# A one-core graph-attention layer: a fourth group of 512 columns turned by DMA, GpSimd's subtraction in quarters, 1 MB loads and another order of exp

## What is computed

```python
q = x @ Wq.T + bq
k = x @ Wk.T + bk
v = x @ Wv.T + bv
scores = q @ k.T / sqrt(128)
scores = where(adj > 0, scores, -9e15)
att = softmax(scores, axis=-1) @ v
att = elu(att)
out = layernorm(x + att, axis=-1, eps=1e-5)
```

## Time and profile before

| | us |
|---|---|
| median of 3 runs | 457.14 |
| the profiled execution | 456.9 |
| span of its trace | 455.1 |
| mean granted TensorE clock | 0.998 |

### The profile page before, as it was taken

The page is one execution under the profiler, slowest core; times in us unless marked ns, Lnnn a source line. Parts: engine busy times, 40 slices in busy tenths (PEclk is TensorE's granted clock), DMA queues, the critical chain, the costliest instruction groups (busy, mean ns, idle before and its releaser), DMA issues.

```text
span 455.1 us, 11786 instructions
## 1 busy us (share of the span) xinstructions
PE 441.7 (97%) x3596; PEld 326.7 (72%) x3596; DVE 376.7 (83%) x665; ACT 354.9 (78%) x643; POOL 273.9 (60%) x426
## 2 busy tenths in 40 slices
PE   7998999999999999999999999999999999999984
PEld 5574677777777777777777777777777777777763
DVE  0678889888898889889898889989898888988633
ACT  3767677778788777778878787778878787777892
POOL 0055336776666666776666666676666666677563
PEclk9999999999999999999999999999999999999999
DMA  8934999899999999999989999999999999995341
GB/s 223 353 94 131 194 238 268 197 257 215 248 234 234 239 213 216 239 241 212 258 229 233 239 225 235 203 252 222 245 225 237 232 227 232 211 254 120 71 78 40
DMA packets 128444, 96.90 MB, mean 213 GB/s; under 512 B 103344, under 2 KB 112048, under 8 KB 128432
## 3 DMA queue, kind: packets, MB, share of 16 engines
q1 hardware_dynamic: 128000, 96.55, 88.4%
q10 hardware_dynamic: 432, 0.20, 0.2%
HBM read 69.47 MB, written 2.10 MB: 157 GB/s over the span
## 4 chain that ended last, share of the span: by engine, by line
PE 90%; ACT 3%; DMA 3%; POOL 2%; issue 1%; SPq 0%; POOLq 0%; DVE 0%; ACTq 0%
PE ps_out L702 23%; PE ps_t L679 14%; PE ps_out L704 12%; PE ps_scores L665 12%; PE ps_scores L664 12%; PE ps_scores L663 12%; PE ps_t L607 2%; DMA p_turned<-p_rows 2%; PE ps_out L618 2%; PE ps_out L607 1%; DMA x_rows<-in_x_dram 1%; ACT scores L399 1%; PE ps_scores L629 1%; ACT p_rows L416 1%; POOL p_rows L289 1%
## 5 line engine op out<-in xcount | busy, mean ns | idle before, releaser
L512 DVE CUSTOM_DVE_ANT_0 scores<-ps_scores,adj 128x1024 f32<-128x1024 f32 x128 | 155.8, 1217 | 1.8 <-issue 0.5
L527 DVE TENSOR_TENSOR p_lo<-ps_t,p_hi 128x512 f16<-128x512 f32 x160 | 108.6, 688 | 49.6 <-ACT p_hi L408 44.5
L408 ACT ACTIVATE p_hi<-ps_t 128x512 f16<-128x512 f32 x160 | 94.8, 593 | 68.6 <-PE ps_t L679 66.5
L399 ACT ACTIVATE scores<-scores,neg_max 128x1024 f32<-128x1024 f32 x128 | 145.8, 1139 | 0.1
L702 PE MATMUL ps_out<-v_parts,p_hi 128*128 128x257 f16 x640 | 124.8, 274 | 0.9 <-DVE p_lo L527 0.8
L704 PE MATMUL ps_out<-v_parts,p_lo 128*128 128x129 f16 x640 | 116.1, 218 | 0.0
L289 POOL TENSOR_TENSOR p_rows<-scores,p_rows 128x1024 f16<-128x1024 f32 x64 | 106.2, 1659 | 11.3 <-ACT p_rows L416 11.3
L498 DVE TENSOR_SCALAR adj<-adj 128x1024 f32<-128x1024 int32 x128 | 108.5, 848 | 0.0
L679 PEld LDWEIGHTS ps_t<-ident,scores 128*128 128x128 f32 x640 | 79.1, 141 | 34.4 <-ACT scores L399 5.4
L679 PE MATMUL ps_t<-ident,scores 128*128 128x128 f32 x640 | 96.4, 273 | 3.3 <-ACT scores L399 3.2
L663 PE MATMUL ps_scores<-k_hi,q_hi 128*128 128x512 f16 x256 | 96.7, 378 | 0.5 <-DVE max_parts L512 0.5
(11 more groups left out here) (70 smaller groups left out, 407.6 us busy)
## 6 DMA issues: line engine op xcount, KB each, us to landing
adj<-in_adj_dram SPq DMA_DIRECT2D x128, 512.0 KB, 4.9
out_dram<-y_out SPq DMA_DIRECT2D x32, 64.0 KB, 4.5
x_rows<-in_x_dram SPq DMA_DIRECT2D x3, 512.0 KB, 6.5
p_turned<-p_rows SPq DMA_TRANSPOSE x64, 5.3
x_rows<-in_x_dram SPq DMA_DIRECT2D x2, 256.0 KB, 3.9
w_rows<-in_L_gnn_Wk_dram ACTq DMA_DIRECT2D x1, 64.0 KB, 2.8
w_rows<-in_L_gnn_Wq_dram ACTq DMA_DIRECT2D x1, 64.0 KB, 3.4
w_rows<-in_L_gnn_Wv_dram ACTq DMA_DIRECT2D x1, 64.0 KB, 3.9
```

The costliest lines, as they stand in the source:

```text
L399: nc.scalar.activation(s_sb[s][:, cols], s_sb[s][:, cols], ACT.Exp, bias=neg_max[:, s:s + 1]).then_inc(exp_done, 1)
L408: nc.scalar.activation(p_hi[:, k, :], ps_t[bank_of(s, g)][:, :], ACT.Copy).then_inc(phi_ready, 1)
L512: nc.vector.tensor_tensor_reduce(out=s_sb[s][:, cols], in0=ps_scores[c % 2][:, :], in1=mask_sb[s][:, cols], scale=SCALE, scalar=-3.0e38, o ...
L527: nc.vector.tensor_tensor(p_lo[:, k, :], ps_t[bank_of(s, g)][:, :], p_hi[:, k, :], ALU.subtract).then_inc(plo_ready, 1)
```

## The change

- `DMA_COLS` becomes 1024 and 1024, so group 3 goes the DMA's way and TensorE turns groups 4 to 7. `T_AT`, `PV_ORDER` and `EXP_ORDER` are set anew: exp runs over pieces 2, 0, 1, 3, and `values` takes groups 4 to 7 first.
- `low_rows` makes each subtraction in four instructions of 256 columns.
- `adj` is loaded in halves of 2048 columns (1 MB); the second half of tile p+1 and the first of tile p+2 are asked for in period p, each behind a DMA transpose.
- `turn` of `c = 1` is issued one period later in SP's order, at the head of a period.
- ACT's `high_rows` move to j = 4 and 6, its end-of-tile steps to j = 1, 3, 5, 7.
- POOL's order is `finish_att`, `low_rows` 0, `finish_y`, `finish_mean`, `low_rows` 1, `finish_norm`.
- DVE finds the row maximum before the mask piece that follows; one mask piece moves to the next period.
- At the start: 12 warm-up transposes for 9, and `x` in six chunks for five.

```diff
-DMA_COLS = (PIECE, BANK,)
+DMA_COLS = (PIECE, PIECE)
-T_AT = {3: 4, 4: 6, 5: 7, 6: 8, 7: 10}
-PV_ORDER = (3, 4, 5, 6, 0, 7, 1, 2)
+T_AT = {4: 3, 5: 5, 6: 8, 7: 9}
+PV_ORDER = (4, 5, 6, 7, 0, 1, 2, 3)
+EXP_ORDER = (2, 0, 1, 3)
+LOW_PARTS = 4
-WARM_UP = 9
-X_CHUNKS = ((0, 1), (1, 2), (2, 4), (4, 6), (6, 8))
+WARM_UP = 12
+X_CHUNKS = ((0, 1), (1, 2), (2, 3), (3, 4), (4, 6), (6, 8))
...
+            def load_half(i, slot, h, first):
                 if not first:
-                    sp.wait_ge(masked_ready, PIECES * (i - 2) + c + 1)
+                    sp.wait_ge(masked_ready, PIECES * (i - 2) + 2 * h + 2)
+                cols = slice(2 * h * PIECE, 2 * (h + 1) * PIECE)
+                sp.dma_start(adj_sb[slot][:, cols], adj_tiled[i, :, cols]).then_inc(adj_in[slot][h], 16)
...
# SP, period(p, n)
-                load_piece(p + 1, 1 - n, 3), store(p - 4, n), load_piece(p + 2, n, 0), load_piece(p + 2, n, 1)
-                turn(p - 1, 1 - n, 0), load_piece(p + 2, n, 2), turn(p - 1, 1 - n, 1)
+                turn(p - 2, n, 1), load_half(p + 1, 1 - n, 1), store(p - 4, n)
+                turn(p - 1, 1 - n, 0), load_half(p + 2, n, 0)
...
# POOL
-                nc.gpsimd.tensor_tensor(p_rows[c][:, w:], s_sb[s][:, c * PIECE:c * PIECE + w], p_rows[c][:, 0:w],
-                                        ALU.subtract).then_inc(rows_lo, 1)
+                for b in range(LOW_PARTS):
+                    cols = slice(b * w // LOW_PARTS, (b + 1) * w // LOW_PARTS)
+                    last = nc.gpsimd.tensor_tensor(p_rows[c][:, w:][:, cols], s_sb[s][:, c * PIECE:c * PIECE + w][:, cols],
+                                                   p_rows[c][:, 0:w][:, cols], ALU.subtract)
+                last.then_inc(rows_lo, 1)
...
# POOL, period(p, n)
-                    finish_y(p - 3, 1 - n, first)
+                    finish_att(p - 3, 1 - n)
                     low_rows(p - 1, 1 - n, 0)
-                    finish_norm(p - 3, 1 - n)
+                    finish_y(p - 3, 1 - n)
+                    finish_mean(p - 3, 1 - n)
                     low_rows(p - 1, 1 - n, 1)
+                    finish_norm(p - 3, 1 - n, first)
...
# ACT, period(p, n)
-                    if j == 0 and has_3:
-                        attention(p - 3, 1 - n)
-                    if j == 2 and has_1:
+                    if j == 4 and has_1:
                         high_rows(p - 1, 1 - n, 0, not warm and p == 1)
-                    if j == 4 and has_1:
+                    if j == 6 and has_1:
                         high_rows(p - 1, 1 - n, 1, not warm and p == 1)
                     if j % 2 == 1 and has_1:
-                        exp_piece(p - 1, 1 - n, j // 2)
-                    if j == 2 and has_3:
+                        exp_piece(p - 1, 1 - n, EXP_ORDER[j // 2])
+                    if j == 1 and has_3:
+                        attention(p - 3, 1 - n)
+                    if j == 3 and has_3:
                         elu_exp(p - 3, 1 - n)
-                    if j == 4 and has_3:
+                    if j == 5 and has_3:
                         row_sum(p - 3, 1 - n)
-                    if j == 6 and has_3:
+                    if j == 7 and has_3:
                         square_sum(p - 3, 1 - n)
...
# DVE, period(p, n)
+                    if j == 7 and has_scores:
+                        row_max(p, n)
-                        if makes_mask:
-                            mask_piece(p + 1, 1 - n, j // 2)
+                    if j == 1 and has_scores:
+                        mask_piece(p, n, 3)
+                    if j in (3, 5, 7) and has_scores and makes_mask:
+                        mask_piece(p + 1, 1 - n, j // 2 - 1)
...
# PE, period(p, n)
-                    if j < 7 and has_2:
-                        values(p - 2, n, PV_ORDER[j + 1], False)
-                    if j == 7 and has_1:
-                        values(p - 1, 1 - n, PV_ORDER[0], not warm)
+                    if has_2:
+                        values(p - 2, n, PV_ORDER[j], first)
```

More of the change, by code:

```diff
@@ L121, in attention_kernel @@
         v_lo = sem("v_lo")
-        adj_in = [[sem(f"adj_in{n}_{c}") for c in range(PIECES)] for n in range(2)]
+        adj_in = [[sem(f"adj_in{n}_{h}") for h in range(2)] for n in range(2)]
         mask_ready = sem("mask_ready")
@@ L191, in exp_count @@
         def exp_count(i, c):
-            return PIECES * i + c + 1
+            return PIECES * i + EXP_ORDER.index(c) + 1
         def bank_of(s, g):
@@ L209, in _ @@
             sp.dma_start(bv_rows[:, :], bv.rearrange("(a d) -> a d", a=1).to_broadcast([P, D])).then_inc(bv_in, 16)
[L211 removed]
+            def load_half(i, slot, h, first):
                 if not first:
[L214 to L216 removed]
+                    sp.wait_ge(masked_ready, PIECES * (i - 2) + 2 * h + 2)
+                cols = slice(2 * h * PIECE, 2 * (h + 1) * PIECE)
+                sp.dma_start(adj_sb[slot][:, cols], adj_tiled[i, :, cols]).then_inc(adj_in[slot][h], 16)
             def load(i, slot):
[L219 to L220 removed]
+                for h in range(2):
+                    load_half(i, slot, h, True)
             def store(i, slot):
@@ L230, in turn, with period @@
                 sp.dma_start_transpose(p_turned[c][s][:, :, :], p_rows[c][:, :]).then_inc(turned[c], 16)
-            def period(p, n, head=True, turns=True, stores=True, loads=True):
+            def period(p, n, head=True, turns_0=True, turns_1=True, stores=True, loads=True):
+                if turns_1:
+                    turn(p - 2, n, 1)
                 if head:
-                    load_piece(p + 1, 1 - n, 3, False)
+                    load_half(p + 1, 1 - n, 1, False)
                 if stores:
                     store(p - 4, n)
[L238 to L242, removed]
+                if turns_0:
                     turn(p - 1, 1 - n, 0)
                 if loads:
-                    load_piece(p + 2, n, 2, False)
-                if turns:
-                    turn(p - 1, 1 - n, 1)
+                    load_half(p + 2, n, 0, False)
             load(0, 0)
             load(1, 1)
-            period(0, 0, head=False, turns=False, stores=False)
-            period(1, 1, stores=False)
+            period(0, 0, head=False, turns_0=False, turns_1=False, stores=False)
+            period(1, 1, turns_1=False, stores=False)
             period(2, 0, stores=False)
@@ L260, in _ @@
             period(TILES, 0, head=False, loads=False)
-            period(TILES + 1, 1, head=False, turns=False, loads=False)
+            period(TILES + 1, 1, head=False, turns_0=False, loads=False)
             store(TILES - 2, 0)
@@ L317, in finish_norm @@
                                         ALU.add).then_inc(pool_done, 1)
+            def finish_norm(i, s, first):
+                one = slice(s, s + 1)
+                base = POOL_OPS * i
                 pool.wait_ge(sqsum_ready, i + 1)
@@ L324, in finish_norm @@
                 pool.wait_ge(pool_done, base + 10)
+                if not first:
+                    pool.wait_ge(stored[s], 8 * (i - s))
                 nc.gpsimd.tensor_tensor(y_out[:, s, :], centred[:, s, :], rstd[:, one].to_broadcast([P, D]),
@@ L575, in period @@
                             low_part(p - 1, 1 - n, g)
+                    if j % 2 == 1 and has_scores:
+                        masked_piece(p, n, j // 2, not warm and p < 2)
+                    if j == 7 and has_scores:
+                        row_max(p, n)
                     if j == 7 and has_2 and not last:
                         reciprocal(p - 2, n)
-                    if j % 2 == 1 and has_scores:
-                        masked_piece(p, n, j // 2, not warm and p < 2)
-                        if makes_mask:
-                            mask_piece(p + 1, 1 - n, j // 2)
-                    if j == 7 and has_scores:
-                        row_max(p, n)
+                    if j == 1 and has_scores:
+                        mask_piece(p, n, 3)
+                    if j in (3, 5, 7) and has_scores and makes_mask:
+                        mask_piece(p + 1, 1 - n, j // 2 - 1)
             for n in range(AHEAD):
                 low_of_projection(n)
-                if n >= AHEAD - PIECES:
-                    mask_piece(0, 0, n - AHEAD + PIECES)
+                if n > AHEAD - PIECES:
+                    mask_piece(0, 0, n - AHEAD + PIECES - 1)
             period(0, 0, has_1=False, has_2=False, warm=False)
@@ L706, in values, with period @@
                 last.then_inc(pv_done, 1)
-            def period(p, n, has_scores=True, has_1=True, has_2=True, warm=True):
+            def period(p, n, has_scores=True, has_1=True, has_2=True, warm=True, first=False):
                 for j in range(STEPS):
@@ L732, in _ @@
             pe.wait_ge(v_lo, STEPS)
-            period(2, 0)
+            period(2, 0, first=True)
             period(3, 1)
```

18 lines of the change are left out of this document (9 added, 9 removed).

## The result

The changed kernel takes 535.77 us (median of 4 runs, 535.07 to 536.91) where the kernel before takes 457.10. The ratio is 1.173, 95% interval 1.170 to 1.175: 79 us slower. The prediction was 519.3 us, with a range of 488 to 544. The trace shows the loop that it forecast. A fall of TensorE's clock, which it didn't name, adds 22 us, and smaller errors the other way take 5 us off; so the sum is 18 us short.

The account below looks back on a forecast made before the run. PE's stream, 12.76 us a period, was taken as the bound. high_rows 0 ending at 68.5, 28 turns of 14.77, one of 14.13, then 15.4 and 5.65 gave a span of 517.3, so 519.3 us; range 488 to 544.

Parts of the forecast that it names:

- The turn: From ACT's high_rows 0 through POOL's quarters, y, row_sum and PE back to high_rows 0: 14.13 us, 14.77 with a meeting.
- the meeting: On POOL, a mask piece waits for the last quarter and holds res back by 0.64 us a turn.
- POOL's other stretch: low_rows 1, the norm, att, then elu_exp: some 0.2 us under the turn, adding nothing.
- the other three mask pieces: On DVE beside POOL: they fall into POOL's gaps or its 0.2 us of slack.
- The last turn: At the end of the loop, where no mask is made: one turn of 14.13 us.
- PE's own period: PE's stream alone would need 12.32 us a period, against 12.76 before.
- The gain of the moved group: One group of transposes per tile leaves PE: 0.44 us, 32 times, 14.1 us if nothing else got late.
- Quarters: POOL's four 256-column instructions per subtraction: 2.58 us, bounds 2.14 and 2.80.
- The start: Smaller x chunk saves 0.8 us of PE's wait; period 3 begins at 60.8 us.
- PE as the bound: Rival: ACT takes the wait in its stride and PE's 12.32 us stays the period; 445.1 us, chance 0.08.
- Late loads: Rival: adj's 1 MB load behind a transpose lands late, costing about 1 us a period; 548 us, chance 0.07.
- the second rival: Mask pieces and quarters on POOL: no meeting, 501.4 us, or two, 537; 0.64 us each a turn; chance 0.27.

Follow-up runs that it names:

- e1: The changed kernel with one move on GpSimd, finish_y ahead of the first low_rows: 442.4 us, ratio 0.971 to the kernel before.
- e3: The changed kernel with 16 dummy transposes of the identity on TensorE before it waits for exp of piece 3: 515.3 us.
- e5: The changed kernel with each low_rows subtraction as one instruction of 1024 columns, no quarters: 496.8 us.
- e2: The changed kernel with ACT's row_sum moved behind the second high_rows at j = 6: 486.7 us.
- e9: e3 with mask piece 1 of every tile cut to 8 of its 1024 columns, so it computes something else: 503.0 us.
- e7: e1 with 9 warm-up transposes for 12, x still in six chunks: 443.6 us.

## Why the prediction was right, and where its size was off

**The turn: right in its order, and partly lucky in its length.** The deciding step, that the subtraction ahead of `y` closes a turn through ACT and POOL that is longer than PE's own stream, is shown by e1: moving that one call opens it. TensorE's way around was 14.77 in the sum; the trace gives 14.53, of which 0.44 is the meeting, so 14.09 for 14.13 without it. But the fast turns are 14.68 to 14.74, because POOL's other stretch closes them. The prediction had that stretch 0.2 us under TensorE's and counted the other three mask pieces into gaps and slack. Two of them lengthen it by 0.48 and 0.44, and it ends 0.15 us later instead. That the whole turn is within 0.1 of 14.77 is two errors that cancel: a meeting put 0.2 too high, and 0.15 of the others left out. The last turn, 13.67 us, is no measure of the 14.13: TensorE makes no scores in it, and part of it is at the low clock (in e3 it is 13.30).

**The range: luck in part.** Its upper end, 544, was made from a second meeting and quarters of 0.70 us. What took the time from 513 or so up to 535.8 was the clock, for which the range had nothing.

**PE's own period: right.** 12.32 counted, 12.31 in e1. The gain of the moved group, 0.45 us a period or some 13 us, exists and is about what e1 is faster than the kernel before (13.6).

**Quarters: right in size, and worse than the sum says in effect.** 2.56 for 2.58 (its own terms add up to 2.57). The cost of the meeting was 0.44 for 0.64. The sum let the mask piece run for its whole 0.69 behind the quarter, and `res` for its whole 0.46 behind the piece; in the trace the quarter ends at 317.51, the piece 0.55 later and `res` 0.31 after that. The rule of the Trainium skill that I weighed ("SBUF — State Buffer", "SBUF: two separate sides": an exclusive lock for the whole instruction) agrees with the second subtraction of e5, which a mask piece waits out to its end. What I drew from it, 0.64 on POOL's path for each piece that quarters let in, does not: the second subtraction loses 0.48 us with quarters, and undivided POOL loses 0.45 in `var` behind it. The quarters cost by their own 0.42 us.

**The clock: missed.** The sum has no term for it, though it says that PE waits 2 to 3 us a period. 15 turns of the 29 are 1.5 us longer by it: 22 us. I had taken that TensorE's clock stays where it was, as in the kernel before, whose page has no slice under 9; but that kernel's PE never stood still in the steady state, so its trace couldn't tell. e3 shows it: with the wait filled, 20.5 us go.

**The start: too careful.** Period 3 began at 58.2 us (59.53 of ACT's first copy in it, less 1.36), not 60.8. Setting the terms side by side: start -2.6, turns at the full clock -2.1, clock +22.4, tail +0.1; 17.8 us together, from a span of 517.3 to 535.1. Without the clock's term, the changed kernel would take some 513 us; e3, where the clock stays up, takes 515.3.

**The rivals.** PE as the bound (445.1 us) did not occur in the changed kernel; its number is nearly that of e1, for which it was in effect worked out. Late loads did not occur: a load of 1 MB lands in 5.7 us (median) instead of the 9.8 I allowed:

```profile
adj<-in_adj_dram SPq DMA_DIRECT2D x64, 1024.0 KB, 5.7
```

A second and a third meeting did occur, on POOL's other stretch: they cost 0.15 us a turn, not the 0.64 of the second rival, because most of their length falls into the slack of that stretch.

**What stays open.** Why the clock falls in every second turn or so and not in all. All 14 waits of 2.09 us and more (up to 2.42) were followed by a slow stretch, but of the 15 waits from 1.96 to 2.04 us only two were: the length of the wait goes with it and doesn't decide it alone. In e2 and e5, with waits of 1.2 to 1.6 us in the steady state, it never fell there. The share of the smaller `x` chunk at the start is open too.

## What to carry to other kernels

When a reordering puts a long operation of engine B ahead of a short one that engine A waits for, look for the loop before looking at busy shares: write down one full turn with start-to-start spacings, and compare it with the period of the bound engine. An engine's idle time is slack only for a chain that doesn't pass through the waits it is made of. Where two ways around are within a few tenths of a microsecond of each other, count the waits on both: small delays on the shorter one can make it the longer. And give TensorE's clock a term of its own as soon as a change lets TensorE stand still for some 2 us in each period; a wait of 2 us then cost 3.5 in this kernel, while waits of 1.2 to 1.6 cost only themselves.

## What the runs showed of the hardware

- The granted clock fell to 0.51 behind idle stretches of 2.0 to 2.4 us in half of the periods; a window of 3.5 us held 19 matmuls there and 32 at the full clock. The 29 turns hold 16 slow stretches, 14 of them behind a wait of 2.09 us or more. With 16 dummy transposes in the gap (0.4 us of idle left) it stayed up.
- Four subtractions of 256 columns on GpSimd take 2.56 us from end to end, one of 1024 takes 2.14.
- A mask piece of VectorE that meets a GpSimd instruction lengthens the next one by 0.44 us, whether that is `res` (the changed kernel; 0.46 without the piece in e9) or `expm1` (e5). Behind an undivided subtraction the piece itself took 1.47 us instead of 0.69.
- The trace's record of the granted clock begins at 13.3 us in the kernel before and at 7.7 in e7, where TensorE's pace doubles (a 512-column projection from 0.85 us to 0.43); a clock of 1.00 read ahead of that is not a measurement.
- The transposing DMA of 2048 columns lands in 4.3 us in the median of the changed kernel, where the mix of 2048 and 1024 took 5.3 before, with loads of other sizes queued around it.
